# Taking the maximum over the gathered rows by halves in a four-layer graph network on one Trainium2 core

## The reference

```python
vals, idx = jax.lax.top_k(scores, S)            # S = 25, scores = -index where adjacent
feats = jax.vmap(lambda x, i: x[i])(X, idx)     # gather: 8 x 1024 x 25 rows of 128 channels
feats = jnp.where(valid[..., None], feats, neg_inf)
agg = feats.max(axis=2)
agg = jnp.where((degree <= S)[..., None], jnp.maximum(agg, 0.0), agg)
h = jnp.concatenate([X, agg], axis=-1)
out = jax.nn.relu(jnp.einsum('bnf,fo->bno', h, W) + b)
```

## Time and profile before

| | us |
|---|---|
| median of 3 runs | 2069.22 |
| lowest, highest | 2068.86, 2071.86 |
| the profiled execution | 2056.89 |
| its span, first to last instruction | 2055.2 |

### The profile page before, as it was taken

The page is one execution under the profiler, slowest core; times in us unless marked ns, Lnnn a source line. Parts: engine busy times, 40 slices in busy tenths (PEclk is TensorE's granted clock), DMA queues, the critical chain, the costliest instruction groups (busy, mean ns, idle before and its releaser), DMA issues.

```text
span 2055.2 us, 28031 instructions
## 1 busy us (share of the span) xinstructions
PE 1570.2 (76%) x9086; PEld 1179.2 (57%) x9086; DVE 1439.9 (70%) x3518; ACT 680.9 (33%) x1372; POOL 1358.2 (66%) x1358
## 2 busy tenths in 40 slices
PE   4666678796778787796788887796788887695777
PEld 3444466474665576474665666464665666474645
DVE  6645688776886688767876688767876788745531
ACT  4011123523244323533244323533244322522252
POOL 5753477777777776777777777777777777771000
PEclk9888978898899978998889988998889978997899
DMA  4111122423233322333224322333224321311010
GB/s 149 40 54 48 50 70 73 123 82 93 71 90 114 112 72 68 111 93 92 71 71 133 95 90 71 109 92 92 71 70 133 105 78 51 110 53 45 1 62 11
DMA packets 79675, 165.44 MB, mean 81 GB/s; under 512 B 24477, under 2 KB 41770, under 8 KB 79530
## 3 DMA queue, kind: packets, MB, share of 16 engines
q0 software_dynamic: 42752, 87.64, 15.7%
q1 hardware_dynamic: 36778, 75.98, 11.2%
HBM read 159.33 MB, written 4.19 MB: 80 GB/s over the span
## 4 chain that ended last, share of the span: by engine, by line
PE 31%; DVE 27%; POOL 14%; DVEq 10%; issue 9%; ACT 7%; DMA 1%; POOLq 0%; ACTq 0%
POOL gathered L426 13%; PE spare L689 9%; DVEq L65 7%; PE big L775 5%; DVE pooled L1024 4%; DVE probs_t L1128 4%; PE side L872 3%; DVE keys L962 3%; PE big L856 3%; DVE hot L1053 2%; PE big L846 2%; DVEq L967 1%; PE big L889 1%; PE big L822 1%; ACT adj_t L457 1%
## 5 line engine op out<-in xcount | busy, mean ns | idle before, releaser
L426 POOL DMA_INDIRECT gathered<-in_x_dram,rows x1336 | 1354.6, 1014 | 502.7 <-issue 432.5
L689 PE MATMUL spare<-hot,x_part 128*128 128x512 f32 x1056 | 313.1, 457 | 53.0 <-DVE best_t L1064 43.8
L1024 DVE TENSOR_REDUCE pooled<-gathered 128x128 f32<-128x2816 f32 (+1 forms) x64 | 304.0, 4749 | 40.3 <-DMA gathered<-in_x_dram,rows 38.1
L689 PEld LDWEIGHTS spare<-hot,x_part 128*128 128x128 f32 x1056 | 233.3, 227 | 117.8 <-DVE best_t L1064 51.4
L775 PE MATMUL big<-values,probs_t 128*128 128x129 f32 x2048 | 246.2, 283 | 0.0
L775 PEld LDWEIGHTS big<-values,probs_t 128*128 128x128 f32 x2048 | 243.1, 199 | 4.9
L1053 DVE TENSOR_SCALAR hot<-running 128x2048 fp32r<-128x2048 bf16 x132 | 159.2, 1233 | 82.0 <-PE spare L689 64.7
L1128 DVE SCALAR_TENSOR_TENSOR probs_t<-row_gain,col_gain,adj_t 128x1024 f32<-128x1024 f32 x128 | 158.0, 1304 | 22.9 <-ACT row_gain L508 22.9
L1175 DVE TENSOR_REDUCE neg_max<-big 128x1 f32<-128x1024 f32 x64 | 77.7, 1222 | 125.2 <-PE big L859 124.7
L856 PE MATMUL big<-xt,row_gain 128*128 128x512 f32 x256 | 134.4, 651 | 34.3 <-ACT adj_less L451 20.0
L872 PEld LDWEIGHTS side<-recip_diag,work 128*128 128x128 f32 x1024 | 128.3, 201 | 52.9 <-issue 43.2
(11 more groups left out here) (169 smaller groups left out, 2289.2 us busy)
## 6 DMA issues: line engine op xcount, KB each, us to landing
adj_in<-in_adj_dram SPq DMA_DIRECT2D x128, 512.0 KB, 3.6
gathered<-in_x_dram,rows POOLq DMA_INDIRECT x1336
xs<-in_x_dram SPq DMA_DIRECT2D x8, 512.0 KB, 4.2
out_dram<-xs SPq DMA_DIRECT2D x8, 512.0 KB, 3.3
w_sb<-in_L_gnn_W_dram SPq DMA_DIRECT2D x1, 128.0 KB
w_sb<-in_L_gnn_W_dram SPq DMA_DIRECT2D x2, 64.0 KB
probs_t<-in_L_gnn_W_dram SPq DMA_DIRECT2D x1, 64.0 KB
gat_w<-in_L_gnn_W_dram SPq DMA_DIRECT2D x1, 64.0 KB
```

The costliest lines, as they stand in the source:

```text
L426: rows_gathered[t % RING].raised_by(pool.indirect_dma_start(out=gathered[:, t % RING, k * C:(k + 1) * C], out_offset=None, in_=x_rows, in_ ...
L689: last = nc.tensor.matmul(spare[:, :], x_parts[part][:, m, :], hot[c][:, j, :], start=(m == 0 and part == 0), stop=(m == T - 1 and part == ...
L1024: link(nc.vector.tensor_reduce(pooled[:, t, :], gathered[:, t % RING, 0:n * C].rearrange("p (k c) -> p c k", k=n), AX.X, ALU.max))
```

## The change

`pool_tile` gets a loop in front of the `tensor_reduce`. As long as more than three rows are left, the upper half of them is merged into the lower half with a two-operand maximum in place, whose operands are both contiguous float32 in SBUF. With an odd count the middle row stays as it is. With 22 rows the steps are 11, 5 and 3 rows wide (22 to 11 to 6 to 3 rows), which is 1408, 640 and 384 elements per partition, and the `tensor_reduce` then runs over 3 rows instead of 22. With 13 rows (graph 0) they are 6, 3 and 2 rows wide, and it runs over 2 rows. Each step has a drain behind it.

```diff
                 dve.wait_ge(ring.sem, ring.at(b, (t // RING + 1) * n))
                 if t == 0 and not (isinstance(b, int) and b == 0):
                     dve.wait_ge(pooled_turned.sem, pooled_turned.at(b, 0))
+                while n > 3:
+
+                    rest = n - n // 2
+                    low_rows, high_rows = gathered[:, t % RING, 0:(n - rest) * C], gathered[:, t % RING, rest * C:n * C]
+                    link(nc.vector.tensor_tensor(low_rows, low_rows, high_rows, ALU.max))
+                    n = rest
                 link(nc.vector.tensor_reduce(
                     pooled[:, t, :], gathered[:, t % RING, 0:n * C].rearrange("p (k c) -> p c k", k=n), AX.X, ALU.max))
```

## The result

The changed kernel takes 2110.35 us (median of 4 runs, 2109.99 to 2110.67). The kernel before, run beside it, takes 2069.04 us (4 runs, 2057.76 to 2071.86). The ratio is 1.0224 with a 95% interval of 1.0195 to 1.0253: slower by 2.2%. Forecast were 2121 us, range 2084 to 2136, and slower with 0.85.

A forecast was written before the change was run, and what follows sets the result against it. POOL's gather stream was taken to set the pace. 64 - 9.3 - 0.8 - 0.2 = +54 us on the 2069.2 us median gives 2123; with holds of 62 us the forecast was 2121 us, range 2084 to 2136.

The forecast's parts named there:

- What bounds the kernel: POOL's gather stream sets the pace from 244 to 1862 us; less DVE work helps only through four waits and the last tile.
- The holds: Gathers starting beside the new maxima in pool_tile are delayed 1.17 us per tile, over 55 tiles 64 us.
- the prediction's rule: A gather starting while DVE runs an instruction with two SBUF operands ends 0.82 us after that instruction.
- The waits: POOL's four waits at tile 1, whose pooling frees the buffer for tile 4, go and give back 9.3 us.
- DVE's saving per tile: Pooling a tile of 22 rows on DVE takes 4.22 us instead of 4.99, 0.77 us less.
- Head and tail: Before graph 1's first gather, 0.2 us gained by an earlier loop start; after the last gather, 0.8 us by faster last-tile pooling.
- The sum: Whole kernel: 64 - 9.3 - 0.8 - 0.2 = +54 us on the profiled execution, 2056.9 to 2111 us.
- the stretch: From the loop's first gather at 243.84 us to the last at 1861.46, 1618.6 us in which gathers set the pace.
- The lower rivals: Three cases below the forecast: no holds 2062 us (0.12), partial hold 2084 (0.10), DVE pays instead 2081 (0.04).
- the maxima do hold: Against the rival that the new maxima delay no gather, leaving 7.2 us of relief: 2062 us, chance 0.12.
- each tile's hold is whole: Against the rival of one delay of about 0.45 us per tile and no second: +15, 2084 us, chance 0.10.
- DVE doesn't pay: Against the rival that maxima wait for running gathers, making a tile 0.6 us longer: near 2081 us, chance 0.04.

The follow-up runs named there:

- The pair with equal DVE length: Kernel before plus the first maximum, or plus an equally long contiguous reduction, ahead of the unchanged reduction over 22 rows: 2141.38 us and 2086.41 us.
- the seven profiles: One profile each: before, changed, 16 rows reduced only, first maximum or contiguous reduction before all 22 rows, first maximum then 11 rows, maxima in pieces; spans 2048.4 to 2142.3 us.

## Why the prediction was right, step by step

**What bounds the kernel**: right. With 74 us less DVE work and no further holds the kernel gained 11 us, and the changed kernel's four waits at tile 1 are gone while DVE waits 117.9 us for gathers.

**The holds**: right in mechanism and size. Forecast 64 us by mean phases and 62 by the phases of the trace; measured 59.0 at the maxima and 60.7 in all. The parts are 0.79 us for the first maximum (0.87) and 0.28 for the third (0.30), with one held gather per tile at each and none at the second, as forecast. The pair with equal DVE length shows the cause. Also right was the reading of the earlier trace rows: of the 112 gathers that start beside the products of line 1128 the first in each of 14 chains is held, and the other 98 start in the last 0.08 us of one product, in 84 cases with the next one already begun, and are not. What the prediction's rule left out changes nothing in its sum: it speaks of two SBUF operands only, while the largest holds before, 37.2 of 71.2 us, are beside line 1053, which has one.

**The waits**: the four, 9.3 us in all, were forecast to go, and they went.

**DVE's saving per tile**: mis-sized without consequence. The strided reduction over 3 rows was taken at 958 ns, a straight line through the shapes of 13 and 22 rows. It took 594, near the lower bound of 550. The line does not hold for few rows: 427 ns for 2, 594 for 3, 2569 for 11, 3672 for 16. That is 1.30 ns per element from 2 to 3 rows, 1.93 from 3 to 11 and 1.72 from 11 to 16. So a tile saved 1.15 us rather than 0.77, which went into DVE's waits for gathers.

**Head and tail**: forecast -0.2 and -0.8, measured +6.5 and -4.2. The +6.5 begins ahead of any changed instruction, with a lower granted clock; the same two parts move by up to 14 and 8 us among the seven profiles. Of the -4.2 the pooling of the last tile explains 1.15.

**The sum**: +54 forecast on the profiled execution, 2111; the changed kernel's profiled execution took 2110.67. That this fits to 0.3 us is luck in part: in the stretch, which the mechanism covers, 54.7 us were forecast (52.7 with the holds taken one by one) and 51.5 came, and head and tail, forecast at -1.0, made up for it with +2.3. The 10.7 us by which 2121 missed come mostly from the base. I added the +54 to a median of three runs that all lay at the upper end of what this kernel does: 13 later runs on one chip lie between 2057.54 and 2069.66 with a median of 2062.79. The changed kernel's runs lie within 0.7 us. Between the medians of the runs made side by side the change is +41 us, between the two profiled executions +54; the spread of the kernel before leaves the size open between these, but not the sign. The lower rivals fell: the maxima do hold, each tile's hold is whole, and DVE doesn't pay (1624 ns for the first maximum on average against 1.63 us forecast; only five paid, 0.03 to 0.06 us each).

## What to carry to other kernels

An engine whose busy share is a third below full can still set the pace: add the fixed gap between its instructions, and look for what it waits for before trusting a share. Before replacing a slow instruction by faster ones, ask what they share with the engine that does set the pace: here a slow reduction of one operand was harmless to the gathers, and quicker maxima of two SBUF operands held two gathers per tile. If such instructions are needed beside gathers, cut them short, since a gather mostly waits only for the rest of the one that is running: that took the holds from 59.0 us to 19.1 here, though it didn't make the change pay.

## What the runs showed of the hardware

- A gather that starts while DVE runs an instruction with two SBUF operands ends 0.81 to 0.82 us after it, in place of 0.94 us after its own start; the longest beside the new maxima took 2.39 us. A gather that is already under way when such an instruction begins is not held, even if it started only 0.01 us earlier (none of 30 beside line 1028). So DVE and POOL are not tied together by semaphores alone: no semaphore stands between line 1028 and the gathers that it holds.
- Line 1053 has a single operand (2048 elements, bf16 in and fp32r out) and holds gathers too, in a second way. Besides those that start in it, it holds gathers that are already under way when it begins, and they end 0.12 us after it. In the timeline before, the gather at 440.93 starts beside a maximum that reads PSUM and wouldn't be held by it, but line 1053 begins 0.18 us later:

```profile
440.50 0.69 DVE L1064 TENSOR_TENSOR best_t<-best_t,spare 128x512 f32<-128x512 f32 x1 [3.21 <-PE spare L689]
440.93 1.51 POOL L426 DMA_INDIRECT gathered<-in_x_dram,rows  x1 [0.30 <-issue]
441.11 2.36 DVE L1053 TENSOR_SCALAR hot<-running 128x2048 fp32r<-128x2048 bf16 x2
```

  In the seven profiles of the table all 105 gathers that had started at most 0.51 us before a one-hot instruction, with nothing else to hold them, were held so, and none of the 45 that had started 0.51 to 0.94 us before. Why a gather is open to this for its first 0.51 us, and to a two-operand instruction at its start only, isn't shown.
- The Trainium skill, SBUF — State Buffer, "Who interferes with whom", says that a DVE instruction with two SBUF inputs contends with GpSimd's reads; the pair of 1048 and 1016 ns agrees. Its inference that a tensor_tensor leaves a DMA from that engine alone does not hold for these gathers.
- On some chips the kernel before ran at 2053 to 2072 us; on others it took 3118 to 3186 us. The kernels profiled there (no profile of the kernel before was taken on such a chip) have much the same busy time on DVE and POOL (1430.9 and 1301.6 us with tile 1 pooled first, against 1439.9 and 1358.2 before), PE is busy for longer (1771.4 against 1570.2 us), and all engines have long idle stretches, a large part of which the profile puts down to nothing it can name. A page of such a chip (tile 1 pooled first), the chain that ended last:

```profile
PE 36%; another core or an unknown queue 23%; issue 19%; DVE 9%; ACT 6%; DVEq 5%; DMA 0%; SPq 0%; ACTq 0%
```

  Why is open. It matters here since the bound is another one there.
